# Self- and causal attention: where the maxima's split, the normalisation, the token-order product and the projection stand in the tick order

## The reference, cut to what matters

```python
scores = einsum('bskgd,bswkd->bskgw', Q, K_win) * scale   # 16 query heads, 4 key heads, all 100 positions
attn   = softmax(where(valid, scores, -inf), axis=-1)
out    = einsum('bskgw,bswkd->bskgd', attn, V_win).reshape(B, S, 128)
return out @ Wo.T
```

```python
sm   = einsum('nlhd,nshd->nlhs', q, k) / sqrt(8)
sm   = softmax(where(causal_mask, -inf, sm), axis=-1)
attn = einsum('nlhs,nshd->nlhd', sm, v).reshape(N, L, 128)
return attn @ Wo.T + bo
```

## Time and profile before

| what | value |
|---|---|
| timed runs: median (lowest to highest) | 1182.33 us (1182.02 to 1182.77) |
| the profiled execution's own time / its span | 1173.58 / 1171.8 us |
| busy share of the span: TensorE matmul, weight load | 78%, 49% |
| busy share: VectorE, ScalarE, GpSimd | 65%, 49%, 22% |
| mean granted TensorE clock | 0.837 |
| L0a: granted clock 21.90 to 52.62 / 52.62 to 90.17 us | 0.50 / 1.00 |
| L1x: granted clock 513.42 to 547.55 / 547.55 to 588.51 us | 0.50 / 1.00 |
| L0a: first reduction starts, last residual ends | 19.1, 89.96 us |
| L1x: first reduction starts, last residual ends | 510.98, 588.26 us |

### The profile page before, as it was taken

One profiled execution on the slowest core, in us unless ns is written; L12 is line 12 of the kernel. 1 busy time (PEld: TensorE's weight loads), 2 busy tenths in 40 slices (PEclk: granted clock), 3 DMA queues, 4 the chain that ended last, 5 costly groups with the idle time before them and its releaser, 6 DMA issues. The chain is left out here.

```text
span 1171.8 us, 18505 instructions
## 1 busy us (share of the span) xinstructions
PE 919.5 (78%) x6163; PEld 569.5 (49%) x6163; DVE 756.2 (65%) x2181; ACT 571.3 (49%) x1660; POOL 255.0 (22%) x349
## 2 busy tenths in 40 slices
PE   4985499999878356179865889794686999999986
PEld 2345499999746222134543358564582233333323
DVE  6457667777658299354477635632547888888823
ACT  3236367777541311132353434462252677777773
POOL 4006245555400022122202000033400111111100
PEclk8697699999979677566966679797695899999997
DMA  9500000000000620100001000543022011111000
GB/s 228 151 1 1 0 2 2 1 2 2 1 1 1 83 30 0 28 1 1 1 1 51 0 1 1 146 128 96 12 46 63 1 26 25 26 26 21 1 2 14
DMA packets 76176, 35.83 MB, mean 31 GB/s; under 512 B 35226, under 2 KB 74561, under 8 KB 76082
## 3 DMA queue, kind: packets, MB, share of 16 engines
q1 hardware_dynamic: 73714, 33.61, 12.8%
q0 software_dynamic: 896, 0.63, 0.2%
q10 hardware_dynamic: 1472, 0.41, 0.2%
HBM read 24.42 MB, written 11.05 MB: 30 GB/s over the span
## 5 line engine op out<-in xcount | busy, mean ns | idle before, releaser
L519 ACT ACTIVATE L3x_E<-L3x_pS 128x400 f32<-128x400 f32 (+1 forms) x384 | 167.8, 507 | 48.6 <-PE L3x_pS L613 47.6
L435 DVE TENSOR_REDUCE L3x_NMP<-L3x_pM 128x1 f32<-128x361 f32 x384 | 178.1, 524 | 18.7 <-PE L3x_pM L591 17.8
L591 PE MATMUL L3x_pM<-ctx_tm 64*128 64x361 bf16 x384 | 104.4, 341 | 14.0 <-DVE L3x_NMP L435 9.0
L613 PE MATMUL L3x_pS<-ctx_tm 64*128 64x400 bf16 (+1 forms) x384 | 107.6, 350 | 3.4 <-ACT L3x_E L519 2.1
L1465 ACT ACTIVATE L0x_E<-L0x_E,ctx_r 128x100 f32<-128x100 f32 x288 | 105.1, 369 | 9.3 <-DVE L0x_E L1372 9.3
L628 PE MATMUL L3x_pO<-L3x_E,CT 128*32 128x400 f32 (+1 forms) x768 | 85.2, 516 | 0.0
L591 PEld LDWEIGHTS L3x_pM<-ctx_tm 64*128 64x128 bf16 x384 | 30.4, 96 | 110.2 <-DVE L3x_NMP L435 90.8
L1554 PE MATMUL L0x_pU<-ctx_tm,L0x_E 128*100 128x129 f32 x576 | 70.5, 279 | 3.1 <-POOL L0x_E L1285 3.1
L1544 PE MATMUL L0x_pS<-L0x_QS,CT 128*128 128x100 f32 x576 | 70.4, 280 | 0.0
L1554 PEld LDWEIGHTS L0x_pU<-ctx_tm,L0x_E 128*100 128x100 f32 x576 | 67.2, 171 | 4.6 <-POOL L0x_E L1285 4.1
L1285 POOL TENSOR_TENSOR L0x_E<-L0x_E,L0x_RZ 128x1200 f32<-128x1200 f32 x24 | 52.6, 2193 | 75.0 <-DVE L0x_RZ L1392 75.0
(11 more groups left out here) (631 smaller groups left out, 2132.6 us busy)
## 6 DMA issues: line engine op xcount, KB each, us to landing
ctx_tm<-in_ctx SPq DMA_DIRECT2D x8, 704.0 KB
ctx_tm<-key_terms SPq DMA_DIRECT2D x16, 270.8 KB, 4.2
key_terms<-ctx_tm SPq DMA_DIRECT2D x42, 90.2 KB
ctx_tm<-in_L_ffn_wi SPq DMA_DIRECT2D x4, 512.0 KB, 7.6
ctx_tm<-in_L_ffn_wo SPq DMA_DIRECT2D x4, 512.0 KB, 7.7
ctx_tm<-query_terms SPq DMA_DIRECT2D x16, 75.0 KB, 3.4
slots_in<-L2a_zeros SPq DMA_DIRECT2D x8, 129.0 KB
L2f_XS<-slots_in SPq DMA_DIRECT2D x4, 258.0 KB, 3.0
```

What stands on the lines that cost most here:

```text
L435: nc.vector.tensor_reduce(NMP[:, p, i // NC4, a, i % NC4:i % NC4 + 1], v, AX.X, ALU.max, negate=True).then_inc(s_mr, 1)
L519: nc.scalar.activation(E[0:r, n % EB, :], pS[0:r, n % 3, 0:NG * T], ACT.Exp, scale=SCALE8).then_inc(s_e, 1)
L591: nc.tensor.matmul(pM[:, n % 3, 0:CW], key_rows(QS, a)[:, b, p, 128 * x:128 * x + 128], key_rows(KS, a)[:, b % KB, c, p, :], start=True, s ...
L613: nc.tensor.matmul(pS[0:NW[k], n % 3, 0:NG * T], key_rows(KS, a)[:, b % KB, k % 4, p, 128 * (k // 4):128 * (k // 4) + NW[k]], key_rows(QS, ...
```

## The change

The tick constants move token_major and normalised from 2b + 9 to 2b + 10, turn and outT from 2b + 10 to 2b + 11, project and residual from 2b + 11 to 2b + 12; stats goes with them to 2b + 13, and there is one tick more. In the loops of VectorE and TensorE the calls stand in another order: residual and project are issued first in their tick, ahead of maximum and max_scores; normalised stands in one loop with split, out_copied and stats in the next; turn stands in one loop with turn_maxima, and token_major and weigh have loops of their own. ScalarE's loop is unchanged in text and takes its tick for outT from the constant.

```diff
-        S_AT, NT_AT, PV_AT, TM_AT, TURN_AT, PROJ_AT = 5, 3, 8, 9, 10, 11
+        S_AT, NT_AT, PV_AT, TM_AT, TURN_AT, PROJ_AT = 5, 3, 8, 10, 11, 12
...
                 for t in range(LAST + 1):
+                    for b in range(B):
+                        if t == 2 * b + PROJ_AT:
+                            residual(b)
                     if t < N:
                         maximum(t)
...
                     for b in range(B):
                         if t == 2 * b + 1:
                             split(b)
+                        if t == 2 * b + TM_AT:
+                            normalised(b)
+                    for b in range(B):
                         if t == 2 * b + PV_AT:
                             out_copied(b)
-                        if t == 2 * b + TM_AT:
-                            normalised(b)
-                        if t == 2 * b + PROJ_AT:
-                            residual(b)
                         if t == 2 * b + PROJ_AT + 1 and b < B - 1:
                             stats(b)
...
                 for t in range(LAST + 1):
+                    for b in range(B):
+                        if t == 2 * b + PROJ_AT:
+                            project(b)
                     if t < N:
                         max_scores(t)
...
                     for b in range(B):
                         if t == 2 * b + NT_AT:
                             turn_maxima(b)
-                    for b in range(B):
-                        if t == 2 * b + PROJ_AT:
-                            project(b)
                         if t == 2 * b + TURN_AT:
                             turn(b)
+                    for b in range(B):
                         if t == 2 * b + TM_AT:
                             token_major(b)
+                    for b in range(B):
                         if t == 2 * b + PV_AT:
                             weigh(b)
```

## The result

The change made the kernel **slower: 1208.37 us** median (1205.39 to 1215.27, 6 runs). The kernel before, timed beside it, had 1181.08; the ratio is **1.026** (95% interval 1.023 to 1.030). (The ratios in this document are those on record for the timed runs; the quotient of the two medians would be 1.023, the low end of that interval.) I had forecast 1190.2 with a range to 1195. The sign was right, the size was off by more than three times.

The account below looks back on a forecast made before the run. No engine full; a chain through VectorE and TensorE bounds each 5.88 us pair of ticks. The change makes pairs 6.35: +3.7 us in L0a, +4.2 in L1x, +7.9 on 1182.33 gives 1190.2, range 1185 to 1195.

Parts of the forecast that it names:

- Even tick 3.00: TensorE's even tick runs back to back, scores, token-major product and weighted output: 3.00 us where it was 2.44.
- odd tick 3.35: Odd tick lasts 3.35 us: 3.07 until OT is copied and TensorE starts, then projection 0.28.
- the transpose ahead of the turned maxima: In ticks 11, 13, 15 and 17 the transpose comes first and puts 0.24 us ahead of the turned maxima.
- projection right after OT's copy: The projection waits for ScalarE's OT copy, TensorE idle about 1.3 us with the next scores queued behind it.
- token_major(0): Start of L0a's pipeline: the first token-major product, moved out of tick 9, starts at 52.07 us.
- The own price of the change: Both attention stages together: +3.7 us in L0a and +4.2 us in L1x, +7.9 in all.
- The step that failed: Clock in both stages: at 2.4 GHz after the first low stretches to the loops' end, so high-clock durations carry the sum.
- late-clock rival: The clock rises only after tick 10 because tick 9 loses its product: 4.1 us more, 1194.3; chance 0.19.
- The other gap: TensorE idle about 1.3 us in the odd tick, ahead of each projection, waiting for OT.
- OT in time: Rival: OT ready before TensorE reaches the projection, odd tick 2.04 instead of 3.35, 1177.1 us; chance 0.06.

Follow-up runs that it names:

- g2: Changed kernel plus five idle 128-row products in tick 9 and ahead of each projection from tick 12 on; 1.003 of the kernel before, 1183.91 us.
- g1: Changed kernel plus five idle 128-row products in tick 9 only, the wait for OT left as it is; 1.023 of the kernel before, 1203.05 us.
- e1: Changed kernel with the transpose at the head of its odd tick and the copy to OT first in ScalarE's order; 1.019 of the kernel before, 1190.54 us.
- g3: Kernel before plus three idle 128-row products at the end of each of ticks 2 to 8; 0.992 of the kernel before.
- h1: Kernel before plus four extra VectorE copies out of PSUM ahead of each residual, lengthening TensorE's wait to 1.37 us; 1.018 of the kernel before.
- h2: Changed kernel plus two idle 128-row products ahead of each projection from tick 12 on, none in tick 9; 1.014 of the kernel before.
- e4: Kernel before plus two extra VectorE copies out of PSUM ahead of each residual, lengthening TensorE's wait to 0.97 us; 1.006 of the kernel before.
- e3: Changed kernel with the transpose behind the turned maxima in the odd tick instead of ahead of them; 1.025 of the kernel before.
- e2: Changed kernel plus five idle 128-row products ahead of each projection from tick 12 on, none in tick 9; 1.014 of the kernel before, 1186.39 us.

## Why the prediction was wrong

Its steps on order and waits held. Even tick 3.00 (2.99), odd tick 3.35 (3.36), the transpose ahead of the turned maxima (65.37, 65.51), projection right after OT's copy, 1.45 us idle where I had about 1.3, token_major(0) at 52.46 for 52.07 in a stage that began 0.39 us later: all as worked out. The own price of the change with the clock stretches of the kernel before is 7.3 us by g2's profile and 0.5 to 7.3 by its timed ratio, for 7.9.

The step that failed is the first paragraph's: the clock is at 2.4 GHz "afterwards to the end of the loops", so "durations at the high level carry the sum". I took the clock of the kernel before for a property of the stage; it changes with what TensorE does there. What the runs showed in its place: 68 and 61 us of the two stages at the low clock where the kernel before has 31 and 34, and 17.4 us that come back when the waits for OT are filled (g1 less g2).

Against the late-clock rival I wrote that "the gap is no larger than the ones that the high level outlives". That holds for the gap it speaks of, the 0.5 us of tick 9, beside 0.29 and 0.58. The other gap of the same prediction, 1.3 us in one piece ahead of each projection, I never held against those numbers. The rival's own part came true: with the stages' later start of 0.39 and 21.22 us, its 55.8 and 553.55 for tick 11 become 56.2 and 574.8, and the trace has 56.12 and 574.68. But it asked only when the clock rises, never whether it falls again, and its price (4.1) is a seventh of the 27.6 us that the sum lacks in the two stages.

The 35.5 us of the two stages, by differences of single profiles: 7.3 the wait's own (g2 less before), 17.4 the falls (g1 less g2), and 10.8 what g1 leaves, that is the later rise and L1x's longer first stretch, 41.0 us for 30.7 (changed less g1). The last term is the weakest: about 4 us of it are L1x's start, where executions of the same code differ as much, and the timed ratios of the two kernels (1.026 and 1.023) overlap. The remaining 3.4 of the 38.9 lie in the other stages and weren't followed.

The rival "OT in time" was mispriced: it left out that scores wait for the exponentials of the tick before. In e1, with the wait for OT gone, a pair of ticks takes 5.92 us, no less than the 5.88 before, so nothing of its 1177 was there to win. Its odd tick of 2.04 was right.

The Trainium skill ("TensorE: Matmul & The Clock Gate", What's actually happening) says that activity releases the throttle and that the throttled state is the default. This case's runs agree in direction: products whose results nobody reads took 9.1 and 8.3 us off the stages between g1 and g2 and sped up the kernel before in g3.

**What stays open.** What exactly brings the clock down. h1 kept it high for 41 us of L0a with TensorE busy 30.55 of 40.80 us, while the changed kernel lost it after 7.15 of 10.05, and e1 after 17.64 of 20.20 with its waits of 1.06 us. The closest pair is h2 and e4, here in L0a from the rise to the next fall:

```profile
57.20:74.10 16.90, 14.04 (x121) 8.09 (x116) 11.22 (x30) 6.31 (x12) 0.00 (x0) 0.99 0.01 1
...
51.30:85.20 33.90, 27.66 (x215) 13.79 (x213) 20.38 (x68) 11.59 (x21) 0.00 (x0) 1.00 0.09 21
```

The longest waits are 0.95 and 0.97 us and the busy shares 83% and 82%; h2, in the new order, lost the clock at 73.7, and e4, in the old one, at 85.6. The amount of idle time alone doesn't tell these apart. The distribution of work over the ticks, its kind, or chance between executions may matter; there is one profile of each kernel, and no run here separates them.

## What to carry to other kernels

Before pricing a new wait on TensorE in durations of the high clock, ask whether the clock survives it: here a wait that costs at most 7 us by itself brought 17 more through falls of the clock (g1 less g2), and more through its later rise. The wait stands ahead of all of TensorE's other work of the tick; putting the instruction that needs the last engine's result behind that work is the obvious thing to try, but no run here did. And where TensorE waits anyway, at the low clock, unused products can pay for themselves: 0.8% of the program in g3, with products of 128 rows, the only height tried.

## What the runs showed of the hardware

- Three unused 128-row products per tick in ticks 2 to 8 ended a low stretch of 30.7 us after 17.1. In the kernel before TensorE was busy for 25.49 of those 30.72 us, for the greater part with 32-row score products, and the clock stayed low.
- Executions of one program differ together with their mean granted clock: e3's from 1188.60 us at 0.838 to 1205.64 at 0.824, h1's from 1191.55 at 0.839 to 1204.57 at 0.826.
- At the low clock ticks 17 and 18 of L0a took 10.40 us (changed kernel), at the high clock 6.32 (e2).
- With longest waits of 0.97 us in e4 TensorE held the high clock for 34 us of L0a; with 0.95 us in h2, in the other order of ticks, for 17.
